# Where the pair loop's large matrix product waits for the output banks: one wait on all banks, or one wait for each bank

## The reference, cut to what matters

```python
x = x + _L0_ffn_ref(_L0_cond_ref(x, cond_512, ...), L0_ffn_identity)
x = x + _L1_ffn_ref(_L1_cond_ref(x, cond_512, ...), L1_ffn_W_base, ...)

# cond_ref: four convolutions over L (same, upsample, same, downsample), weights scaled per batch element
# L0_ffn:  y = einsum('bsd,ed->bse', x, identity)
# L1_ffn:
y = jnp.einsum('bth,oh->bto', x, W_base) + b_base
z = jnp.einsum('bth,erh->bter', x, A)
contribs = jnp.einsum('bter,eor->bteo', z, Bm) * SCALING
alpha = jax.nn.softmax(jnp.log(prior + EPS) + logits / GAMMA, axis=-1)
return y + jnp.einsum('bteo,bte->bto', contribs, alpha)
```

## Time and profile before

| | us |
|---|---|
| median of 3 runs | 1635.23 |
| lowest, highest | 1633.67, 1635.56 |
| the profiled execution | 1632.8 |
| its span, first to last instruction | 1630.7 |
| PE busy / PEld busy | 1569.9 (96%) / 1378.5 (85%) |
| DVE busy | 798.7 (49%) |
| ACT busy | 576.4 (35%) |
| POOL busy | 206.4 (13%) |
| mean granted TensorE clock, share of full | 0.996 |
| mean DMA share | about a third of 16 engines |

### The profile page before, as it was taken

The page is one execution under the profiler, slowest core; times in us unless marked ns, Lnnn a source line. Parts: engine busy times, 40 slices in busy tenths (PEclk is TensorE's granted clock), DMA queues, the critical chain, the costliest instruction groups (busy, mean ns, idle before and its releaser), DMA issues.

```text
span 1630.7 us, 25362 instructions
## 1 busy us (share of the span) xinstructions
PE 1569.9 (96%) x8503; PEld 1378.5 (85%) x8503; DVE 798.7 (49%) x2061; ACT 576.4 (35%) x1291; POOL 206.4 (13%) x280
## 2 busy tenths in 40 slices
PE   5999999999999999999989999999999999999998
PEld 4688888888888888888869999999999999989988
DVE  7744655444444443444464445445445445445443
ACT  3323433333333333333333333333333333333332
POOL 1101101011101111111101011011011011011010
PEclk9999999999999999999999999999999999999999
DMA  4343232333233333333342333333233233233231
GB/s 101 107 104 101 83 91 64 103 77 103 77 103 77 103 89 91 89 91 99 89 135 79 90 77 94 86 77 97 83 77 98 82 77 100 80 77 103 77 77 65
DMA packets 54331, 145.66 MB, mean 89 GB/s; under 512 B 17233, under 2 KB 19345, under 8 KB 54306
## 3 DMA queue, kind: packets, MB, share of 16 engines
q1 hardware_dynamic: 53616, 144.96, 32.6%
q10 hardware_dynamic: 690, 0.37, 0.1%
HBM read 111.75 MB, written 33.55 MB: 89 GB/s over the span
## 4 chain that ended last, share of the span: by engine, by line
PE 88%; DVE 6%; issue 3%; ACT 1%; DMA 1%; DVEq 0%; POOL 0%; SPq 0%; POOLq 0%
PE bank L1094 28%; PE bank L1096 27%; PE bank L1095 27%; PE bank L1358 3%; DVE xout L851 3%; PE bank L1240 1%; DMA xraw<-x_dram 0%; PE bank L1304 0%; DMA win<-in_L_cond_weights_dram 0%; PE bank L1275 0%; DVE fw_l L879 0%; PE bank L1294 0%; DVE mtmp L660 0%; PE bank L1364 0%; DVE win L902 0%
## 5 line engine op out<-in xcount | busy, mean ns | idle before, releaser
L1094 PE MATMUL bank<-fw_h,ct_h 128*128 128x512 f32 (+2 forms) x1280 | 464.0, 363 | 27.7 <-DVE xout L851 27.7
L1095 PE MATMUL bank<-fw_l,ct_h 128*128 128x512 f32 (+2 forms) x1280 | 450.2, 352 | 0.0
L1096 PE MATMUL bank<-fw_h,ct_l 128*128 128x512 f32 (+2 forms) x1280 | 449.4, 351 | 0.0
L343 POOL TENSOR_TENSOR x_l<-xraw,x_h 128x512 fp32r<-128x512 f32 x128 | 166.0, 1318 | 1296.4 <-ACT x_h L483 1296.4
L1094 PEld LDWEIGHTS bank<-fw_h,ct_h 128*128 128x128 f32 x1280 | 240.8, 188 | 58.7 <-DVE xout L851 23.2
L987 DVE TENSOR_TENSOR ct_l<-bank,ct_h 128x384 fp32r<-128x384 f32 (+1 forms) x256 | 96.1, 416 | 390.7 <-ACT ct_h L531 390.3
L1096 PEld LDWEIGHTS bank<-fw_h,ct_l 128*128 128x128 f32 x1280 | 241.1, 188 | 22.6
L1095 PEld LDWEIGHTS bank<-fw_l,ct_h 128*128 128x128 f32 x1280 | 241.5, 189 | 16.6
L1094 PE MATMUL bank<-x_h,tw 128*128 128x512 f32 x640 | 253.2, 396 | 0.0
L1096 PE MATMUL bank<-x_h,tw 128*128 128x512 f32 x640 | 252.8, 395 | 0.0
L1095 PE MATMUL bank<-x_l,tw 128*128 128x512 f32 x640 | 252.1, 394 | 0.0
(11 more groups left out here) (203 smaller groups left out, 1774.8 us busy)
## 6 DMA issues: line engine op xcount, KB each, us to landing
xraw<-in_x_dram SPq DMA_DIRECT2D x32, 512.0 KB, 5.0
xres<-in_x_dram SPq DMA_DIRECT2D x32, 512.0 KB, 3.8
x_dram<-xout SPq DMA_DIRECT2D x32, 512.0 KB, 2.9
xraw<-x_dram SPq DMA_DIRECT2D x32, 512.0 KB, 4.9
xres<-x_dram SPq DMA_DIRECT2D x32, 512.0 KB, 3.9
out_dram<-xout SPq DMA_DIRECT2D x32, 512.0 KB, 2.9
xraw<-in_x_dram SPq DMA_DIRECT2D x32, 511.5 KB, 6.5
xraw<-x_dram SPq DMA_DIRECT2D x32, 511.5 KB, 6.4
```

What stands on the lines that cost most here:

```text
L343: nc.gpsimd.tensor_tensor(x_l[h][:, PAD:PAD + HL], src, x_h[h][:, PAD:PAD + HL].bitcast(F32), ALU.subtract).then_inc(s["x_ready"], 1)
L1094: mm(out, wh, xh, start=start, stop=False, skip_group_check=True)
L1095: mm(out, wh, xl, start=False, stop=False, skip_group_check=True)
L1096: return mm(out, wl, xh, start=False, stop=stop, skip_group_check=True)
```

## The change

`ffn_begin` no longer waits for `ffn_out`. `ffn_chunk` waits instead, at k = 0 of each block, for that block alone. `block_outs(ly, pairs, e)` is the count at which block e of the last of `pairs` pairs is out: blocks x pairs + e + 1, with the initial count of one for each block in it. Nothing else is changed.

```diff
+def block_outs(ly, pairs, e):
+
+    return len(BLOCKS[ly["lora"]]) * pairs + e + 1
...
             def ffn_chunk(ly, j, k, es=(0, 1)):
                 for e in es:
                     cols, _ = block_cols(ly, e)
+                    if not k:
+                        pe.wait_ge(ly["s"]["ffn_out"], block_outs(ly, j, e))
                     last = three(ffn_ps[e][:, 0:cols.stop - cols.start], ctf(ct_h, k), ctf(ct_l, k),
...
             def ffn_begin(ly, j):
                 s = ly["s"]
                 pe.wait_ge(s["ct_ready"], 4 * j + 2)
-                pe.wait_ge(s["ffn_out"], ffn_outs(ly, j))
```

## The result

The changed kernel takes **1593.96 us** (median of 4 runs, 1592.46 to 1594.2), the one before 1634.45 beside it (1632.73 to 1635.56). The ratio is 0.9754, with a 95% interval of 0.9742 to 0.9767: 40.5 us less. The forecast was 1594.3. The profiled span went from 1630.7 to 1592.3, by 38.4. That is less than the medians differ by: the profiled execution of before (1632.8) is near the lowest of its four, and that of the changed kernel (1594.2) is the highest of its four.

A forecast was written before the change was run, and what follows sets the result against it. TensorE, busy 96% of the span, was taken to bound the kernel. Gains of 12.7 + 2.1 + 25.2 + 0.9 = 40.9 us off 1635.2 gave 1594.3 us; range 1590 to 1602.

The forecast's parts named there:

- Parts 1 and 2: First layer's loop, start of the big product: bank 4 waits no more; bank 5's weights 0.02 us late, at no cost.
- Part 3: First layer, `stage_u`: its weight load 0.17 us late for v_l, costing 0.04; gain 0.55 a body, 12.7 over 23 bodies.
- the free 0.13: Lateness of a weight load, in us, taken to cost nothing, from a load 0.21 late that cost 0.08.
- Part 4: First layer outside its loop: stalls at 99, 195 and 806 (layer change) save 0.47 each, at 172 0.69; 2.1 us.
- x loads run two pairs ahead: First layer: given with the claim that everything after `stage_u` moves with it, for 0.55 us a loop body.
- Part 5: Second layer's loop: bank 4's weights 0.05 us late at no cost, so the whole 0.84 stall goes 30 times; 25.2 us.
- Part 6: Last pair: the product starts after the first result, at 1613.08 instead of 1613.94; gain 0.9 us, 0.5 of 1.38 stays.
- Part 7: Both loops: 106 added instructions for waits against the pair's number, taken to cost 0, bounded at 6.6 us.
- no instruction is gone: Reason given why the added instructions' cost in the loops cannot be below nothing.
- The estimate of 6.6 us: Cost of the 106 added loop instructions at 0.062 us each, if none were hidden; not used in the sum.
- The granted clock is no rival with a price: Whole kernel: clock 1.00 where TensorE is densest, 0.98 only in a stretch with setup work; no cost or chance assigned.

The follow-up runs named there:

- the value alone: Changed kernel, but bank 4's wait asks for all results of the former pair, as before the change; 1633.86 us (10 runs), ratio 0.9997.
- the order of the banks: Changed kernel, but in the first layer's bodies chunk 0 does bank 5 first and bank 4 second; 1606.2 us, ratio 0.9828.
- the kernel with less room: Changed kernel, but `stage_u` in the first layer stands one piece (three matmuls, 0.69 us) earlier; 1610.84 us, ratio 0.9859.
- the kernel with both waits: Changed kernel, but the old full wait stands in `ffn_begin` again, ahead of the waits by bank; 1639.78 us, ratio 1.0034.

## Why the prediction was right

- **Parts 1 and 2**, bank 4's wait gone and bank 5's own free: right. Full stream at both (411.42, 412.11). The gain was undone by the value alone (1633.86) and by the order of the banks (23.02 us a body).
- **Part 3**, v_l late next: the place was right. The load was 0.12 us late and not 0.17, since it followed v_l's end (412.60 + 0.74 = 413.34) by 0.05: the 0.11 that the sum used came from a place where a control instruction stands in between. 0.12 is within the free 0.13, and the 0.04 that it should cost was not there. The free 0.13 itself holds: 0.81 late cost 0.69 in the kernel with less room. So the body gained 0.574, not 0.55; over 23 bodies that is 0.6 us.
- **Part 4**, outside the loop: 1.59 of 1.63 in the written-out bodies. At 172 us the stall fell as said, but not into two short ones: all that stays is 0.29 ahead of bank 4 (`stage_v`'s last matmul at 171.77, the product's second at 172.41, where 0.35 would do), and bank 5's wait there costs nothing. The 0.47 at the layer change is the step that failed. "x loads run two pairs ahead" holds in the loop; at the layer change the load hangs on SP's queue, takes 8.29 us, and is what is late next. About 1 us lost.
- **Part 5**, the second layer: 25.73 for 25.2. All 30 waits are gone, bank 5 and bank 7 begin at 0.16 and 0.17. The other runs with the same second layer have 23.54 to 23.56 us a body for this one's 23.52, so 24.4 to 25.7 is what the term is worth. One reading in it was wrong and did no harm: "0.05 late, under the free 0.13" took the free lateness from a load behind a 512-column matmul. Behind the 256-column matmuls of `stage_v` next to nothing is free (0.60 late cost 0.59, 0.29 late cost 0.29), so 0.05 would have cost some 0.04 each time. The load came in time all the same, for the same reason as in part 3: where nothing stands in between it follows a result by 0.05 and not by 0.11.
- **Part 6**, the last pair: 0.88 for 0.9. The 1.38 of the earlier trace rows is 0.51, as said:

```profile
1575.07 1.35 DVE L856 TENSOR_TENSOR xout<-bank,xres 128x318 f32<-128x318 f32 x3 [1.14 <-PE bank L1246]
1575.71 0.40 PE L1099 MATMUL bank<-fw_h,ct_h 128*128 128x354 f32 x1 [0.51 <-DVE xout L856]
```

- **Part 7**, the added instructions: 0, shown to 1 us by the kernel that keeps them and has the time of before. The trace of the changed kernel shows why: TensorE works its register instructions well ahead of the matmul that they stand before, at 409.96 for the matmul at 411.42, at 410.65 for that at 412.11, and at 1272.29 for that at 1275.05. They cost time only where an unmet wait holds them up together with the matmul. The prediction's "no instruction is gone" was not so: the control instruction that carried the wait for `ffn_out` in the first layer is gone. The distances at the second layer's bank 5 and bank 7:

```profile
1274.89 0.32 PE L1101 MATMUL bank<-fw_h,ct_l 128*128 128x354 f32 x1
1275.05 0.32 PE L1099 MATMUL bank<-fw_h,ct_h 128*128 128x354 f32 x1
...
1279.21 0.32 PE L1101 MATMUL bank<-fw_h,ct_l 128*128 128x354 f32 x1
1279.38 0.32 PE L1099 MATMUL bank<-fw_h,ct_h 128*128 128x352 f32 x1
```

The estimate of 6.6 us from the figure in the Trainium skill ("TensorE: Matmul & The Clock Gate", section "Wait — 56ns, not 53.3ns?") is not borne out: the control instructions are worked while matmuls run. The Trainium skill, "Advanced Engine Details and Errata", section Sequencer Loop, has it that engine instructions are queued and control instructions started by the sequencer. This case agrees with both sides of it: a control instruction in mid-stream is hidden (0.16 us from matmul to matmul), and one behind an unmet wait makes what is behind it later (0.24 for 0.12 us, 0.13 for 0.05).

- **"The granted clock is no rival with a price"** was wrong. The earlier trace rows showed 0.98 over 240 us, and I put it down to setup work; inside lay a stretch at 0.83. It made 1.5 us between the two profiled executions. The start made another 1.2, which isn't the change and doesn't show in the clock: the turn at 95.11 is at 96.26 in the changed kernel, and at 96.32 in the one with the full value, which has the time of before, and the granted clock is 0.83 from 70 to 80 us in all three.

The sum of 40.9 and the medians' 40.5 agree so well in part by luck: about 1 us too much at the layer change stands against about 1 too little in the loops. The 2.6 us that the start and the narrow matmuls took from the profiled gain belong to single executions as far as the runs show; how much of them is in the medians isn't known.

## What to carry to other kernels

A consumer that waits for all of several results can start on the first if it works through them in the order in which they come. The gain is at most the stall itself, at most the distance from the first result to the last, and at most the work that can be done before the last is needed; and waits that are met on arrival showed no price. Before counting such a gain, ask at each place what is late next, on the DMA queues too: here one value was at the edge of free, and one load took the gain of a whole place. Keep control and register instructions out of the place between the wait that is really waited for and the instruction that does the work: there nothing hides them.

## What I had not expected of the hardware

- TensorE's granted clock fell to 0.50 (1.2 GHz) while PE was shown busy for 20 of 20 us. What ran before the fall were matmuls of 32 and 4 columns; spread between matmuls of 512 columns they left it at 1.00, for 4.2 us less from turn to turn. The Trainium skill ("TensorE: Matmul & The Clock Gate", section "HAM oscillation — how this bites in real kernels") warns of gaps in which TensorE is idle. Here there was none in the records, so a busy row is no proof of a full clock.
- How late a weight load may come for nothing depends on the matmul ahead of it. Behind 512-column matmuls, which start every 0.23 us, 0.12 late cost nothing, 0.21 cost 0.08 and 0.81 cost 0.69; behind 256-column ones, every 0.12 us, 0.29 late cost 0.29 and 0.60 cost 0.59. An estimate from these: free is the time from start to start of the matmul ahead, less 0.11 us.
- From the result's end to the weight load that waits for it took 0.05 us with the wait on the load, 0.12 to 0.13 with one control instruction in between, and 0.24 with two. One more of them there in each layer made some 5 of the 5.6 us by which the kernel with both waits is slower than before, while the same instructions in mid-stream cost at most 1 us.
